# Sixth layer's expert matrices loaded and made ternary inside the fourth layer's batch loop

## The reference, cut to what matters

```
def weight_quant(w):
    scale = 1.0 / maximum(mean(abs(w)), 1e-5)
    return clip(round(w * scale), -1.0, 1.0) / scale
...
q = softmax(where(window, (q_nope @ k_nope + q_rope @ k_rope) * s, -1e30))   # fourth layer
...
out = out + combine[:, e] * bitlinear(up * relu(gate) ** 2, down_w[e])       # sixth layer, 8 experts
```

## Time and profile before

| | us |
|---|---|
| median of 3 runs | 2605.31 (2603.61 to 2605.87) |
| the profiled execution | 2603.4 |
| its span | 2601.5 |
| fourth layer | from 1198 to about 1819 |
| sixth layer, matrices made ternary | from 2066 to 2130 |
| sixth layer, experts | from 2130 to the end |

### The profile page before, as it was taken

The page is one execution under the profiler, slowest core; times in us unless marked ns, Lnnn a source line. Parts: engine busy times, 40 slices in busy tenths (PEclk is TensorE's granted clock), DMA queues, the critical chain, the costliest instruction groups (busy, mean ns, idle before and its releaser), DMA issues.

```text
span 2601.5 us, 51149 instructions
## 1 busy us (share of the span) xinstructions
PE 2017.1 (78%) x15486; PEld 1434.8 (55%) x15486; DVE 1865.8 (72%) x5146; ACT 1402.4 (54%) x3709; POOL 491.2 (19%) x573
## 2 busy tenths in 40 slices
PE   4689999999998686565899999998677536555555
PEld 4667777777776564333677777776555323233332
DVE  3357888788787456995777777674577698878887
ACT  1036555565654343443466665665555547666765
POOL 0011121112111000111333333331344350000000
PEclk9999999999999898777899999999688659988988
DMA  2001111111110202000011111110100130000000
GB/s 95 0 20 28 29 32 28 28 30 31 28 29 11 78 1 90 1 1 5 25 30 32 31 29 29 31 33 18 27 10 10 72 130 1 1 1 1 1 1 33
DMA packets 63063, 72.10 MB, mean 28 GB/s; under 512 B 40210, under 2 KB 41939, under 8 KB 60372
## 3 DMA queue, kind: packets, MB, share of 16 engines
q1 hardware_dynamic: 62932, 70.72, 9.2%
HBM read 63.47 MB, written 2.10 MB: 25 GB/s over the span
## 4 chain that ended last, share of the span: by engine, by line
PE 56%; DVE 24%; issue 10%; ACT 7%; DVEq 1%; DMA 1%; SPq 0%; POOL 0%; ACTq 0%; POOLq 0%
PE ps L644 5%; PE ps L615 5%; PE ps L606 4%; PE ps L628 3%; PE ps L676 3%; PE ps L1717 3%; PE ps L1773 3%; PE ps L578 3%; PE ps L1707 2%; PE ps L1756 2%; PE ps L1782 2%; DVE f_ams L2503 2%; PE ps L2136 2%; PE ps L1738 2%; DVE d_ks L1583 2%
## 5 line engine op out<-in xcount | busy, mean ns | idle before, releaser
L361 ACT ACTIVATE a_pr<-ps,a_nm 128x257 f32<-128x257 f32 x512 | 238.1, 473 | 182.7 <-DVE a_nm L475 182.7
L483 DVE COPY a_pT<-ps 128x512 f32<-128x512 f32 x256 | 170.4, 686 | 92.7 <-PE ps L644 92.1
L1537 ACT ACTIVATE d_pr<-d_st,d_nm 128x257 f32<-128x257 f32 x256 | 128.2, 502 | 197.7 <-DVE d_nm L1633 171.5
L2584 PE MATMUL ps<-f_wt,f_nxT 128*128 128x512 bf16 x512 | 157.0, 438 | 87.7 <-DVE f_act L2487 86.0
L475 DVE TENSOR_REDUCE a_nm<-ps 128x2 f32<-128x514 f32 x256 | 174.8, 683 | 0.0
L644 PE MATMUL ps<-ident,a_pr 128*128 128x128 f32 x1024 | 160.4, 279 | 0.0
L1756 PE MATMUL ps<-d_kc,d_qc 128*128 128x257 f32 x512 | 139.9, 396 | 0.0
L2360 ACT ACTIVATE f_rg<-ps 128x512 f32<-128x512 f32 x128 | 75.9, 593 | 117.6 <-PE ps L2584 116.7
L644 PEld LDWEIGHTS ps<-ident,a_pr 128*128 128x128 f32 x1024 | 117.4, 140 | 33.4 <-issue 12.7
L301 POOL TENSOR_TENSOR a_sf<-a_sf,a_ratio 128x256 f32<-128x256 f32 x64 | 39.4, 615 | 507.1 <-DVE a_ratio L504 507.1
L606 PE MATMUL ps<-a_cT,a_wqk 128*128 128x257 f32 x512 | 132.7, 381 | 2.9 <-DVE a_k L449 1.7
(11 more groups left out here) (352 smaller groups left out, 5314.8 us busy)
## 6 DMA issues: line engine op xcount, KB each, us to landing
a_cT<-in_ctx SPq DMA_DIRECT2D x64, 257.0 KB, 2.7
d_cT<-in_ctx SPq DMA_DIRECT2D x64, 257.0 KB, 2.7
f_wf<-in_f_w SPq DMA_DIRECT2D x12, 1024.0 KB, 4.8
a_vbd<-a_vself SPq DMA_DIRECT2D x256, 8.0 KB
e_vb<-e_vs SPq DMA_DIRECT2D x256, 8.5 KB
c_wf<-in_c_w SPq DMA_DIRECT2D x3, 1024.0 KB, 7.4
x_all<-in_x SPq DMA_DIRECT2D x1, 2048.0 KB, 7.8
d_wo<-in_d_wo SPq DMA_DIRECT2D x1, 2048.0 KB
```

The costliest lines, as they stand in the source:

```text
L361: ins = act.activation(pr[j][:, g, :], ps[:, S_BANK[u % 2] + k, S:LK], ACT.Exp, bias=nm[j][:, g:g + 1], accum_out=ssum[j][:, 0, g:g + 1])
L483: dve.tensor_copy(pT[u][:, :, :, :], ps[:, T_BANK[u % 2], :].rearrange("p (g c q) -> p g c q", g=2, c=2))\
L1537: ins = act.activation(pr[j][:, g, :], st[u][:, k, :], ACT.Exp, bias=nm[u][:, k:k + 1], accum_out=sm[j][:, g:g + 1])
L2584: ins = pe.matmul(ps[:, 2 + 2 * k + w, :], lhsT=nxT[s][:, c, :], rhs=wt[:, 3 * e + w, c * IE:c * IE + IE], start=(c == 0), stop=(c == KT - 1))
```

## The change

The quantisation leaves the sixth phase. In the loop of 48 steps of the fourth phase each pair of steps hosts one matrix m. In the first step of a pair (b even) ACT sums the absolute values at the end of its step. In the second (b odd) PE multiplies by the matrix of ones just ahead of the two transposes of `values`; DVE makes the thresholds ahead of its copy in `values_out`, the `below` part between `recip` and `scores_out(b, 1)`, and the `ternary` part at the end of the step. POOL makes none of it. SP loads the first four matrices as the phase begins, and the others in the loop, one for two batches, 512 KB each, into four places.

```diff
@@ fourth phase, SP
+            eng.wait_ge(d_fold_out.sem, d_fold_out.at(1, 0))
+            for m in range(4):
+                eng.dma_start(f_wf[:, m, :], d["f_w"][:, m, :]).then_inc(f_w_loaded[m].sem, 16)
             eng.wait_ge(vt_ready.sem, vt_ready.at(1, 0))
             for b in range(B):
                 j = b % 2
+                m = (b - 7) // 2
+                if b % 2 and 0 <= m < NW - 4:
+                    eng.wait_ge(f_wt_ready.sem, f_wt_ready.at(m, 1))
+                    eng.dma_start(f_wf[:, m % 4, :], d["f_w"][:, m + 4, :]).then_inc(f_w_loaded[m % 4].sem, 16)
@@ fourth phase, ACT, end of step
                 scale(b, j, 0)
+                if hosted and not hosted.second:
+                    act.wait_ge(f_w_loaded[hosted.slot].sem, f_w_loaded[hosted.slot].at(hosted.turn + 1, 0))
+                    act.activation(f_abs[:, hosted.slot, :], f_wf[:, hosted.slot, :], ACT.Abs,
+                                   accum_out=f_asum[:, bass.ds(hosted.m, 1)]).then_inc(f_abs_sum.sem, 1)
@@ fourth phase, DVE
+            def thresholds(m):
+
+                mean = ps[:, T_BANK[1], 2 * P:2 * P + 1]
+                dve.tensor_scalar(f_ws[:, 0, bass.ds(m, 1)], mean, 1.0 / (HID * IE), EPS_W, ALU.mult, ALU.max)
+                dve.tensor_scalar(f_ws[:, 1, bass.ds(m, 1)], mean, 0.5 / (HID * IE), 0.5 * EPS_W, ALU.mult, ALU.max)
+                dve.tensor_scalar(f_ws[:, 2, bass.ds(m, 1)], mean, -0.5 / (HID * IE), -0.5 * EPS_W, ALU.mult, ALU.min)\
+                    .then_inc(f_mean_out.sem, 1)
+
+            def below(m, slot):
+                dve.wait_ge(f_mean_out.sem, f_mean_out.at(m, 1))
+                dve.tensor_scalar(f_neg[:, :], f_wf[:, slot, :], f_ws[:, 2, bass.ds(m, 1)], None, ALU.is_lt)\
+                    .then_inc(f_neg_done.sem, 1)
+
+            def ternary(m, slot):
+                dve.wait_ge(f_neg_done.sem, f_neg_done.at(m, 1))
+                dve.scalar_tensor_tensor(f_wt[:, m, :], f_wf[:, slot, :], f_ws[:, 1, bass.ds(m, 1)], f_neg[:, :],
+                                         ALU.is_gt, ALU.subtract).then_inc(f_wt_ready.sem, 1)
...
-            def values_out(b, j, first):
+            def values_out(b, j, first, hosted=None):
                 dve.wait_ge(v_psum.sem, v_psum.at(b, 1))
+                if hosted and hosted.second:
+                    thresholds(hosted.m)
...
                 recip(b, j, 0)
+                if hosted and hosted.second:
+                    below(hosted.m, hosted.slot)
                 scores_out(b, j, 1, n == 0)
...
+                if hosted and hosted.second:
+                    ternary(hosted.m, hosted.slot)
@@ fourth phase, PE
-            def values(b, j):
+            def values(b, j, hosted=None):
+                if hosted and hosted.second:
+                    pe.wait_ge(f_abs_sum.sem, f_abs_sum.at(hosted.m, 1))
+                    pe.matmul(ps[:, T_BANK[1], 2 * P:2 * P + 1], lhsT=ones[:, :], rhs=f_asum[:, bass.ds(hosted.m, 1)],
+                              start=True, stop=True)
@@ sixth phase: the loads, ACT's sums, POOL's and DVE's part and PE's matmuls are gone
-            for m in range(NW):
-                pe.wait_ge(abs_sum.sem, abs_sum.at(0, m + 1))
-                if m:
-                    pe.wait_ge(mean_out.sem, mean_out.at(0, m))
-                pe.matmul(ps[:, 7, m:m + 1], lhsT=ones[:, :], rhs=asum[:, m:m + 1], start=True, stop=True)\
-                    .then_inc(mean_psum.sem, 1)
-            pe.wait_ge(wt_ready.sem, wt_ready.at(0, NW))
+            pe.wait_ge(f_wt_ready.sem, f_wt_ready.at(NW, 0))
```

More of the change, by code:

```diff
@@ L8 @@
+from collections import namedtuple
 from contextlib import ExitStack
@@ L1352, in build @@
     phase(ternary_ffn)
+    NW, WE = 3 * NE, KT * IE
+    EPS_W = 1e-5
+    f_shelf = Shelf(d_shelf.top)
+    f_wt = f_shelf.put("f_wt", [P, NW, WE], BF16)
+    f_asum = f_shelf.put("f_asum", [P, NW])
+    f_ws = f_shelf.put("f_ws", [P, 3, NW])
+    f_stage = Shelf(116 * 1024)
+    f_wf = f_stage.put("f_wf", [P, 4, WE])
+    f_neg = f_stage.put("f_neg", [P, WE])
+    f_abs = f_stage.put("f_abs", [P, 4, WE], BF16)
+    f_w_loaded = [signal(f"f_w_loaded{j}", 16) for j in range(4)]
+    f_abs_sum, f_mean_out = signal("f_abs_sum"), signal("f_mean_out")
+    f_neg_done, f_wt_ready = signal("f_neg_done"), signal("f_wt_ready")
     def latent_attention(sb):
@@ L1425, in latent_attention @@
         AHEAD = BT + 1
+        Hosted = namedtuple("Hosted", "m slot turn second")
         def steps(eng, step):
@@ L1434, in steps @@
                 for o in range(2 * BT):
-                    step(i * 8 + (BT + o), (BT + o) % 8, i * 2 + (1 + o // BT), i * 4 + (BT + o + 1) // 2)
+                    step(i * 8 + (BT + o), (BT + o) % 8, i * 2 + (1 + o // BT), i * 4 + (BT + o + 1) // 2,
+                         Hosted(i * 4 + o // 2, o // 2, i, o % 2 == 1))
             for b in range(B - 3 * BT, B):
@@ L1462, in window, with step @@
                     .then_inc(wm_ready.sem, 1)
-            def step(b, s, tile, pair):
+            def step(b, s, tile, pair, hosted=None):
                 if not (isinstance(b, int) and b == B - 1):
@@ L1793, in step @@
                     turn(b - 1, 1 - j, 0)
-                values(b, j)
+                values(b, j, hosted)
                 if n < B - 1:
@@ L2403, in vector @@
             dve.wait_ge(wr_loaded.sem, wr_loaded.at(1, 0))
[L2404 to L2424, removed]
-                    dve.wait_ge(neg_done.sem, neg_done.at(0, m // 2 + 1))
-                    behind = neg[:, m // 2 % 2, :]
-                dve.scalar_tensor_tensor(wt[:, m, :], wf[:, m % 8, :], ws[:, 1, m:m + 1], behind,
-                                         ALU.is_gt, ALU.subtract).then_inc(wt_ready.sem, 1)
-                if m + AHEAD < NW:
-                    threshold(m + AHEAD)
-            w3 = ws[:, 0, :].rearrange("p (e k) -> p e k", k=3)
+            wlink_n = chain("f_wlink2", 3)
+            w3 = f_ws[:, 0, :].rearrange("p (e k) -> p e k", k=3)
             wlink_n.link(dve, dve.tensor_tensor(ec[:, 0, :], w3[:, :, 0], w3[:, :, 0], ALU.mult))
```

37 lines of the change are left out of this document (4 added, 33 removed).

## The result

| | us |
|---|---|
| before, median of 4 runs on the same chip | 2604.46 (2599.99 to 2605.87) |
| after, median of 4 runs | 2544.97 (2543.76 to 2551.28) |
| ratio | 0.9786, 95% interval 0.9773 to 0.9798 |
| repeated later: after, 5 runs | 2548.23 (2545.71 to 2553.4), ratio 0.9797 (0.9785 to 0.981) |

I cut both traces at the row in which each layer's statistics are gathered (the `BATCH_NORM_AGGREGATE x16` on DVE) and subtracted. Executions of the kernel after differ by a few us, so the profile of the repetition (span 2545.7) stands beside the first one (2549.1).

A forecast was written before the change was run, and what follows sets the result against it. PE was taken to set the pace in the fourth layer's loop and DVE in the ternary stage. 60.6 us removed and 25.8 added make 34.8 faster: 2568.6 from 2603.4 profiled, stated as 2570, range 2552 to 2590.

The forecast's parts named there:

- All that follows shifts with it ... I put nothing for that: After the removed ternary stage: the experts only start earlier, at the same low PE clock, with 0 us change.
- The gain of 60.6: Sixth layer: with the matrices ready, L2433 follows the reciprocal at 2069.15 instead of starting at 2129.74, saving 60.6 us.
- The added 25.8: Fourth layer's loop: 12 x (0.4 with `project` + 1.75 without) = 25.8 us added.
- PE's matmul: Fourth layer's loop, ahead of `values`: 0.4 us for each matrix, bounds 0.28 to 0.56.
- `below` in steps without `project`: Fourth layer's loop: takes 1.15 us, delays `last_out` with 0.1 slack, and stalls PE by 1.05 us.
- `ternary`: End of steps without `project`: next `scores_out` late by some 0.75 us, of which about 0.3 is left on PE.
- The clock: Rival, fourth layer's loop: PE's clock falls to 0.90, costing another 45 us, 2615; slower from about 0.92 on; 7 in 100.
- Half of a load of 1 MB: SP's 512 KB matrix load, queued ahead of the next context: about 2.6 us, covered by over 2 us of slack.
- POOL holding `below`: Rival, fourth layer's loop: `below` waits for POOL's mask operation, 1.5 us later; 35 us more, 2605; 1 in 10.
- "Nearly all is hidden": Rival, fourth layer's loop: `below` takes 0.75, PE finds other slack, only 10 us of matmuls remain, 2555; 13 in 100.
- Steps with `project` hide the work: Twelve hosting steps: DVE's thresholds, `below` and `ternary` fit into its idle time; only PE's 0.4 us is paid.
- SP and ACT cost nothing: Fourth layer's loop: loads leave the context in time and ACT's sum fits its idle, under 0.1 us to spare for PE.

The follow-up runs named there:

- the kernel with 68 fillers: The changed kernel with 68 one-column DVE memsets at the end of the fourth layer's program: 2550.46 us, ratio 0.9802 to the kernel before.
- 20 fillers: The kernel before with 20 one-column DVE memsets at the end of the fourth layer's program: 2583.47 us, ratio 0.9919 to the kernel before.
- the two-matrix kernel: The changed kernel with one of every four matrices moved from its step without `project` into the next with it: 2539.96 us, ratio 0.9756 to the kernel before.

## Why the prediction was wrong, step by step

**The step that failed** is "All that follows shifts with it ... I put nothing for that". The experts didn't only shift: their 16 tiles became 22 us shorter. The reason that I gave spoke of the clock alone; the place of the loop in DVE's stream had not come to my mind. Fillers alone bring the stalls back in the kernel after (+20.7 in the sixth layer) and take them out of the kernel before (-20.6), so this is shown. The six stalls of 3.1 to 3.3 us are some 20 of the 22 us. It is a property of the kernel before, which had them by the chance of its length; any edit that changes the number of DVE's instructions ahead of the loop could have lifted them. They were there to be read: "<-issue 19.3" in the lines view.

**The gain of 60.6** was right: 64.5 - 3.9.

**The added 25.8** came out at 24.3 in the repetition and 26.8 in the first profile, but not by its terms. That the sum fits is luck: terms that were too large by some 9 us and falls of the clock that weren't in it make up for each other.

- PE's matmul: 0.4 put, 0.20 measured (24 of them 4.8 us, not 9.6). My bounds, 0.28 to 0.56, left it out: the rows' durations overlap their neighbours, and only the distance between starts is what PE pays.
- `below` in steps without `project`: 1.05 put, about 0.65 measured, as it takes 0.73 and not 1.15. The median that I chose comes from rows in which POOL's operation was already running; here DVE starts 0.03 ahead of POOL. I had used this very argument for `ternary`, but not for `below`.
- `ternary`: 0.3 put; 0.54 by itself, and its wait isn't seen in its old place once `below` is there.
- Without a fall the first four of a pair grew by 1.57 and the second by 1.2 (35.66 to 36.87 in the kernel with 68 fillers), forecast 2.15 for both; twelve make about 16.5 us.
- The clock: nothing put, as a rival with 7 in 100 and from 0.92 down. It fell by little, to 0.98 over the loop; 24.3 and 26.8 less 16.5 leave 8 to 10 us for the falls, which happen to fill up what the terms were too large by. The forecast's "PEclk 1.00 in the loop" was wrong, and its own sign of being wrong showed. That rival came true at about a fifth of its price of 45.
- Half of a load of 1 MB was put at 2.6 us (half of 4.8 is 2.4) and took 3.7; the cover held all the same.

**The rivals.** POOL holding `below` did not come about: it starts first, and where it starts inside POOL's mask operation (`below` behind `last_out`) it takes 0.73 to 0.97 and doesn't wait for the end. `below` at the end of the step shows that POOL can hold `ternary`, by 0.8 us in each of twelve steps; that kernel's 47 us are not the price of this alone, as `below` lies in another place too and the clock falls in every four. "Nearly all is hidden" had the right `below`, 0.73 us, but PE still waited.

**Steps with `project` hide the work:** borne out by two matrices in one such step. **SP and ACT cost nothing:** no wait of PE's keys for the context or of the new matmul for ACT's sum in the trace after; the loads of 512 KB landed in 3.7 us, the contexts in 2.8 (2.7 before).

```profile
d_cT<-in_ctx SPq DMA_DIRECT2D x64, 257.0 KB, 2.8
f_wf<-in_f_w SPq DMA_DIRECT2D x24, 512.0 KB, 3.7
```

**The balance:** 2568.6 for the profiled execution, less 21.9 for the tiles, 1.5 for the loop and 3.5 for the ends of the fourth and the fifth layer, and 5.9 more for layers 1 to 3, gives 2547.6; the profiled execution of the repetition took 2547.67.

**What stays open.** It is open why the loop stalls at 2036 and not at 2023 or 2056: the runs give one bad start, four good ones and no mechanism. The tiles' 21.9 us are also 1.3 more than what 20 fillers took out of the kernel before, and no run shows where these lie. It is open, too, why the falls come every 75 us, in every second four; and they don't always: with 68 fillers, which lie behind the loop and leave it as it is, the profiled execution had four, two of 3.4 us and two of 10.2, at 1392, 1515, 1692 and 1733. The number of falls in one execution is thus no measure of a kernel. That they hang on PE's waits is likely (none without `below`, most and longest where PE waits 2.6 us in one piece), but the two-matrix kernel has two falls where the one without `below` has none with PE busy for as long, and the kernel with the matmul three times has no more busy time than the one after. The mean alone doesn't decide, and what does wasn't found.

## What to carry to other kernels

Before changing a kernel, look for idle time put down to issue near the edges of each hardware loop, and try some 20 one-column fillers ahead of it: here a stall that depends on placement was worth more than half of the 35 us that the change itself was to bring, and it makes the difference of two versions say something about neither. The sum alone isn't the sign. In the fourth layer DVE has more of it, 26.3 us in the kernel before, 1.96 at each of six turns of the loop:

```profile
1403.88 0.42 DVE L1629 CUSTOM_DVE_ANT_0 d_st<-ps,d_wm 128x257 f32<-128x257 f32 x1 [1.96 <-issue]
```

There PE sets the pace, and no run shows that it costs anything; in the sixth layer's tiles 86.0 us of PE's idle time are put down to DVE's L2487.

When work is put into an engine's free time, what counts is when its operation starts against those of POOL that it overlaps (`below` kept its 0.73 us where it started 0.03 us ahead, `ternary` lost 0.8 where it started behind), and what the next consumer's idle is at that very place; the 24 operations of 0.73 us (17.5 us of work) cost 16.5 us in one place of the step and 47 more in another. And before the number of clock falls is compared, more than one execution of each kernel is needed. And take the price of a matmul from the distance between the starts of its neighbours, not from its duration.

## What was new about the hardware

- DVE's loop of 276 instructions stalls 3.1 to 3.3 us at each edge when it begins at instruction 2036 of its stream (counted in the program), in two kernels, and not at 1955, 2023, 2056 or 2224.
- A DVE operation that starts 0.03 to 0.05 us ahead of a POOL operation runs at its own speed (0.73, 1.27), and POOL's is longer by 0.56 or 1.09. Started 0.85 us and just behind the start of a POOL operation, `ternary`, with two inputs from SBUF, took 2.07 and 2.13, but 1.28 at 2084.90 in the kernel before, where it started 2.7 us into one; `below`, with one, started 0.53 us into POOL's mask operation, took 0.73 and stretched the mask from 1.08 to 1.52, and took 0.97 where it started 0.66 us into it (the kernel with `below` behind `last_out`).
- The granted clock falls from 2.4 to 1.2 GHz for 3.4 us at a time in the loop, in most executions every 75 us, and for 6.8 to 10.2 us in every four where PE waits 2.6 us in one piece; single falls of 6.8 and 10.2 us stand in other kernels too.
- With an unchanged loop the profiled executions had six, six, five and four of these falls.
